# A fused attention, quantised feed-forward and expert kernel: the attention and expert stages written in new orders, and the first chunk's inputs loaded early

## The chip, the cores and the metric

One core of a Trainium2 chip runs the kernel. The metric is the device time of one execution in microseconds. A core has TensorE (PE, with its weight loads PEld), VectorE (DVE), ScalarE (ACT), GpSimd (POOL) and SyncE (SP). Each engine runs its own list of instructions strictly in the order written; they meet only at semaphores. SP issues all DMAs but a few of the setup.

## The reference

```python
x = x + tanh(g_xattn[0]) * L0_xattn(layernorm(x), ctx)      # 4 heads, one score matrix summed over the batch, |.| >= 1
x = x + tanh(g_ffn[0])   * L0_ffn(layernorm(x))             # rms_norm * gamma, int8-quantised rows, ternary weights, gelu
x = x + tanh(g_xattn[1]) * L1_xattn(ctx, ctx, layernorm(x)) # causal convolution of k*v pairs, times q, 64 groups of 8
x = x + tanh(g_ffn[1])   * L1_ffn(layernorm(x))             # top-6 routing, 6 experts and 2 shared ones, silu(g) * u
```

x and ctx are 16 x 256 x 512 in fp32 (4096 rows of 512), the first feed-forward widens to 2048, an expert to 256. In the first feed-forward a layer norm (mean m, variance v, epsilon 1e-5) is followed by an RMS norm with epsilon 1e-6.

## The kernel before

The 4096 rows are cut into 8 chunks of 512 (four tiles of 128 rows). Four stages follow each other, each in its own block, with all engines meeting between blocks: a setup; the scores stage (`scores_block`), which sums the score matrix over all chunks and writes gates and values of every chunk to DRAM; the attention stage (`attn_block`); the experts stage (`experts_block`). fp32 operands of a product are split in a high and a low part (tile names ending in `_hi`, `_lo`), and `products` (L52) issues three matmuls for one.

**Attention stage**, one chunk q: `retention` (values times scores, half s into `ps_o`), `group_stats`, `group_pow`, `group_shift`, `group_norm` (group norm, into `ao`), `turn_o` (transposes into `ps_r`), `times_gamma`, `gated`, `cut_z`, `project` (output product, `ps_r` again), `add_x` (residual), then for pairs of tiles `pair_variance`, `pair_rms`, `layer_pow`, `pair_shift`, `layer_norm`, `times_gain`, `pair_scale`, `round_y`, `pair_bf16` and a DMA transpose `turn_y`. For each tile j follow `mm1` (four products into three banks `ps_h`), `gelu` per bank, `scale_h` (row maximum), `round_h`, `to_bf16`, a DMA transpose `turn_h`, `mm2` (one bank `ps_y`), `residual` and `store`. The values' high parts are made by `cut_v` (ACT) and the low ones on POOL. Python loops write the stage out in full; in round c the engines work at the feed-forward of chunk c and, interleaved by hand, at the attention of chunk c + 1. The order in a round is the order of the calls, for instance on ACT (L714 to L731):

```python
            gelu(c, 2, (2, 3))
            ...
                for k in range(KT):
                    cut_z(q, k)
            round_h(c, 1)
            if q + 1 < NCH:
                cut_v(q + 1)
            round_h(c, 2)
            gelu(c, 3)
```

Variances are made by `variance` (L59): six small DVE operations on the even and odd halves that bn_stats leaves. `pair_rms` and a second power on POOL give the RMS factor.

**Experts stage**, one chunk q: `turn_x2`, `norm_x`, `turn_q`, `read_q` bring x in; `keys`, `pairs` (POOL), `cut_kv`, `cut_t` prepare 16 `unit`s of the convolution, whose products go to `ps_m` and are multiplied and reduced on DVE (`e_zp`, `e_x3T`); `add_x2`, `turn_x3`, `nat_stats`, `norm_nat`, `turn_xn`, `cut_xn` give the normalised input `e_xn`. Then come 16 steps s (4 shared, 12 routed) of `gate`, `up`, `silu`, `weigh`, `gated`, `cut_hd` and `down`; `gate` and `up` have one PSUM bank each, `down` sums over all steps in `ps_out`. `finish` and `store` end the chunk. Round g does the steps of chunk g and the convolution of chunk g + 1; the table `UNITS` says at which steps the units stand. Each engine's rounds stand in one `Fori` loop (L1167, L1254, L1454, L1661, L1843), so one copy of the code is run again, and DMA addresses and some operands are computed in registers. The first chunk's convolution stands ahead of the loop. The stage begins with the loads of its x, keys (`e_c`), filter (`e_t_raw`) and constants (L1135 to L1147).

## Time and profile before

| what | value |
|---|---|
| median of 3 runs | 2332.93 us (2327.42 to 2332.95) |
| profiled execution, its own time | 2325.81 us |
| its span, first to last instruction | 2324.0 us |
| granted TensorE clock, mean | 0.944 |
| busy share: PE, DVE, ACT, POOL | 87%, 67%, 44%, 41% |
| HBM traffic | 193.26 MB read, 33.69 MB written |

The span is the time from the first to the last instruction of the one profiled execution; the 1.8 us between it and its own time lie around it. Busy shares are means over four stages with different limits, so the stages have to be read apart.

### The profile page before, as it was taken

What the parts mean: (1) busy time and instruction counts of PE and PEld (TensorE: products, weight loads), DVE (VectorE), ACT (ScalarE), POOL (GpSimd) and SP (SyncE); (2) the same over time, 40 slices, a digit from 0 to 9 for tenths busy, and PEclk for the clock granted to TensorE, in tenths of its full rate; (3) what the DMA queues carried; (4) which work ended last, traced back from release to release, by engine and by line L of the source; (5) the groups of instructions that cost most, each with busy time, mean ns of one, the idle gap of its engine ahead of it and who ended that gap; (6) DMA issues with size and microseconds to landing.
All of it is one profiled execution on the core that took longest, in us unless ns stands there. A gap on an engine that the chain in (4) does not pass through costs nothing.

```text
span 2324.0 us, 30136 instructions
## 1 busy us (share of the span) xinstructions
PE 2017.0 (87%) x10162; PEld 1602.5 (69%) x10162; DVE 1546.4 (67%) x2487; ACT 1017.7 (44%) x1414; POOL 952.0 (41%) x775
## 2 busy tenths in 40 slices
PE   5999568887787545799899899899899899899998
PEld 4989444444454234688788788788788788688787
DVE  4776456666666358588578678678578579578511
ACT  3345345555555321633633633633633633443432
POOL 0110133333332021465465465465465465365464
PEclk9999779999999857899999999999999999899999
DMA  6666314443443321322332332332232242232231
GB/s 214 235 217 231 131 54 116 111 105 96 108 118 82 69 66 46 104 85 90 111 95 86 109 103 86 106 106 86 93 119 82 80 124 90 72 113 73 69 136 64
DMA packets 169968, 248.76 MB, mean 107 GB/s; under 512 B 91280, under 2 KB 92688, under 8 KB 163632
## 3 DMA queue, kind: packets, MB, share of 16 engines
q1 hardware_dynamic: 169616, 247.86, 34.3%
q8 instruction: 34, 0.56, 0.1%
q14 instruction: 30, 0.25, 0.0%
q10 hardware_dynamic: 288, 0.10, 0.0%
HBM read 193.26 MB, written 33.69 MB: 98 GB/s over the span
## 4 chain that ended last, share of the span: by engine, by line
PE 43%; DVE 7%; issue 6%; ACT 5%; POOL 3%; DMA 1%; ACTq 0%; SPq 0%; DVEq 0%; POOLq 0%
PE e_ps_u L54 4%; PE e_ps_u L56 4%; PE e_ps_u L55 4%; PE e_ps_m L54 4%; PE e_ps_m L56 3%; PE e_ps_m L55 3%; PE e_ps_out L54 3%; PE e_ps_out L55 3%; PE e_ps_out L56 3%; PE e_ps_g L56 3%; PE e_ps_g L55 3%; PE e_ps_g L54 3%; POOL e_dn_lo L1185 1%; DVE e_kv_lo L1504 1%; DVE e_x3T L1532 1%
## 5 line engine op out<-in xcount | busy, mean ns | idle before, releaser
L1180 POOL TENSOR_TENSOR e_gu_lo<-e_gu_raw,e_gu_hi 128x1024 fp32r<-128x1024 f32 (+1 forms) x128 | 272.8, 2131 | 449.6 <-ACT e_gu_hi L1269 447.3
L1532 DVE TENSOR_REDUCE e_x3T<-e_zp 128x128 f32<-128x1024 f32 x128 | 267.4, 2089 | 4.4
L54 PE MATMUL e_ps_u<-e_xn_hi,e_gu_hi 128*128 128x512 f32 x512 | 205.5, 401 | 4.0 <-DVE e_xn_lo L1554 2.5
L54 PE MATMUL e_ps_out<-e_hd_hi,e_dn_hi 128*128 128x512 f32 x512 | 208.8, 408 | 0.0
L54 PE MATMUL e_ps_m<-e_kv_hi,e_t_hi 128*128 128x288 f32 x592 | 180.7, 305 | 29.7 <-DVE e_kv_lo L1504 22.1
L55 PE MATMUL e_ps_out<-e_hd_lo,e_dn_hi 128*128 128x512 f32 x512 | 205.2, 401 | 0.0
L56 PE MATMUL e_ps_out<-e_hd_hi,e_dn_lo 128*128 128x512 f32 x512 | 205.2, 401 | 0.0
L55 PE MATMUL e_ps_u<-e_xn_lo,e_gu_hi 128*128 128x512 f32 x512 | 203.7, 398 | 0.0
L56 PE MATMUL e_ps_u<-e_xn_hi,e_gu_lo 128*128 128x512 f32 x512 | 203.6, 398 | 0.0
L958 PE MATMUL ps_h<-w1q,ayqT 128*128 128x512 bf16 x512 | 130.3, 403 | 79.4 <-ACT ah L681 71.9
L1203 POOL TENSOR_TENSOR e_kv_raw<-e_ke 128x512 f32<-128x512 f32 x128 | 139.4, 1089 | 125.7 <-DVE e_kv_lo L1504 95.5
L1185 POOL TENSOR_TENSOR e_dn_lo<-e_dn_raw,e_dn_hi 128x512 fp32r<-128x512 f32 x128 | 179.6, 1403 | 6.9 <-ACT e_dn_hi L1275 6.9
L1477 DVE TENSOR_TENSOR e_hd_lo<-e_hd,e_hd_hi 128x512 fp32r<-128x512 f32 x128 | 125.2, 978 | 78.6 <-ACT e_hd_hi L1297 78.6
L56 PE MATMUL e_ps_m<-e_kv_hi,e_t_lo 128*128 128x288 f32 x592 | 177.0, 299 | 0.0
L55 PE MATMUL e_ps_m<-e_kv_lo,e_t_hi 128*128 128x288 f32 x592 | 176.8, 299 | 0.0
L1283 ACT ACTIVATE e_sg<-e_ps_g,vecs 128x512 f32<-128x512 f32 x96 | 66.2, 690 | 242.4 <-PE e_ps_g L56 241.5
L1472 DVE SCALAR_TENSOR_TENSOR e_hd<-e_ps_u,vecs,e_sgw 128x512 f32<-128x512 f32 x96 | 71.7, 747 | 140.7 <-PE e_ps_u L56 116.0
L1297 ACT ACTIVATE e_hd_hi<-e_hd 128x512 fp32r<-128x512 f32 x128 | 80.4, 628 | 190.0 <-DVE e_hd L1472 189.7
L1194 POOL TENSOR_TENSOR e_sgw<-e_sg,e_wb 128x512 f32<-128x512 f32 x96 | 127.1, 1324 | 80.2 <-ACT e_sg L1283 79.5
L958 PEld LDWEIGHTS ps_h<-w1q,ayqT 128*128 128x128 bf16 x512 | 48.4, 101 | 151.1 <-ACT ah L681 87.5
L54 PE MATMUL e_ps_g<-e_xn_hi,e_gu_hi 128*128 128x512 f32 x384 | 152.5, 397 | 0.0
L56 PE MATMUL e_ps_g<-e_xn_hi,e_gu_lo 128*128 128x512 f32 x384 | 151.5, 395 | 0.0
(271 smaller groups left out, 5304.7 us busy)
## 6 DMA issues: line engine op xcount, KB each, us to landing
e_gu_raw<-in_mgu SPq DMA_DIRECT2D x96, 512.0 KB, 3.3
e_dn_raw<-in_md SPq DMA_DIRECT2D x128, 256.0 KB, 3.2
e_wb<-wts SPq DMA_DIRECT2D x8, 1536.0 KB, 6.6
stage<-in_x SPq DMA_DIRECT2D x8, 1024.0 KB, 6.8
c<-in_ctxT SPq DMA_DIRECT2D x8, 1024.0 KB, 5.8
raw_w<-in_w1T SPq DMA_DIRECT2D x8, 1024.0 KB, 4.8
raw_w<-in_w2T SPq DMA_DIRECT2D x8, 1024.0 KB, 7.3
gates<-gate SPq DMA_DIRECT2D x8, 1024.0 KB, 4.8
```

The lines of the kernel that those rows point to most:

```text
L54: nc.tensor.matmul(out, w_hi, x_hi, start=first, stop=False, skip_group_check=skip)
L55: nc.tensor.matmul(out, w_hi, x_lo, start=False, stop=False, skip_group_check=skip)
L56: return nc.tensor.matmul(out, w_lo, x_hi, start=False, stop=last, skip_group_check=skip)
L958: last = nc.tensor.matmul(h_bank(c, j, n)[:], yqT[:, j, k], keep["w1q"][:, k, n * 512:(n + 1) * 512], start=(k == 0), stop=(k == KT - 1))
L1180: nc.gpsimd.tensor_tensor(gu_lo[:, s % 2, a], gu_raw[:, s % 2, a], f32(gu_hi[:, s % 2, a]), ALU.subtract).then_inc(gulo_done, 1)
L1185: nc.gpsimd.tensor_tensor(dn_lo[:, s % 2], dn_raw[:, s % 2], f32(dn_hi[:, s % 2]), ALU.subtract).then_inc(dnlo_done, 1)
L1194: nc.gpsimd.tensor_tensor(sgw[:], sg[:], wb[:, (s - SHARED) // 2], ALU.mult).then_inc(sgw_done, 1)
L1203: nc.gpsimd.tensor_tensor(out[:, :, 0:32].rearrange("p b (d i) -> p b d i", i=CD), view(ke, m * B * EXT, (EXT, B), (0, 4), (1, CD)), view( ...
L1297: nc.scalar.activation(hd_hi[:, s % 2], hd[:], ACT.Copy).then_inc(hdhi_done, 1)
L1472: nc.vector.scalar_tensor_tensor(out=hd[:], in0=ps_u[:], scalar=vecs[:, V_BU + e:V_BU + e + 1], in1=sgw[:], op0=ALU.add, op1=ALU.mult).the ...
L1477: nc.vector.tensor_tensor(hd_lo[:, s % 2], hd[:], f32(hd_hi[:, s % 2]), ALU.subtract).then_inc(hdlo_done, 1)
L1532: nc.vector.tensor_reduce(x3T[:, lb].rearrange("p (b n) -> p b n", b=B)[:, :, hh * CD:(hh + 1) * CD], zv(5, (1, 8), (21, 8)), AX.X, ALU.ad ...
```

## The change

The scores stage keeps its code; its tiles `gate` and `val` now lie in buffers that live through the whole kernel.

- **Attention stage.** All five engines' lists are written anew, each as one loop over i of single calls in which `at(op, c, ...)` issues a call only for an existing chunk. The work of one iteration is taken from three chunks: PE does `mm2` of tiles 1 to 3 of chunk i - 1, `mm1` of chunk i, `turn_o` and `project` of chunk i + 1, and `retention` of chunk i + 2. Work on four tiles or pairs is split in single calls (`gelu` per bank, `layer_norm`, `round_y`, `times_gain` per tile).
- **Small operations.** `variance` is replaced by `bn_aggr` per tile and one tensor_scalar in the attention and experts stages (not in the scores stage). `pair_rms` and the second power go: the scale is ((1 + 1e-6) v + 1e-6 * 1e-5)^-0.5 in one power, v the variance without epsilon. `pair_scale` and `scale_h` lose one operation each.
- **Experts stage.** The `Fori` loops are gone; all rounds are written out, again as one loop over i of single calls. `down` of the last step moves behind the round's end, in front of the next round's `up`; `down_first` splits the first `down` by output block; units stand at other places between the steps; `finish` is called per output block; the DVE part of a unit is split in `multiply` and `add_terms`.
- **Early loads.** `stage`, `o` and `gate` are shared by the stages. In the attention stage's last rounds SP loads the first chunk's keys into `stage` once the last values are cut, its first filter and constants into `gate`, and three quarters of its x rows into `o`. The experts stage then loads only the last quarter, `wroute` and `skipD` before it starts.

```diff
@@ attention, SP
+        def fetch_context():
+            sp.wait_ge(vlo_done, START + NCH)
+            sp.dma_start(early(keep)[1], dram["ctxG"].rearrange("g (k p) n -> g p k n", p=P)[0]).then_inc(early_in, 16)
+        def fetch_constants():
+            rest = early(keep)[2]
+            sp.wait_ge(z_done, START + 4 * NCH)
+            sp.dma_start(rest[:, 0], dram["toep"][0]).then_inc(early_in, 16)
...
+        def fetch_x():
+            sp.wait_ge(oT_done, 4 * NCH)
+            sp.wait_ge(x2_out, START + 16 * TJ * (NCH - 2))
+            for j in range(TJ - 1):
+                sp.dma_start(early(keep)[0][:, j], x2_rows(dram, 0, j)).then_inc(early_in, 16)
@@ attention, DVE: group_stats
-            variance(nc, dve, ostats, omom, ove[:], GN_EPS, omom_done, 12 * q + 6 * s)
+            for b in range(2):
+                nc.vector.bn_aggr(omv[:, b], ostats[:, b]).then_inc(omom_done, 1)
+            dve.wait_ge(omom_done, 6 * q + 3 * s + 2)
+            nc.vector.tensor_scalar(ove[:], omv[:, :, 1], GN_EPS, None, ALU.add).then_inc(omom_done, 1)
@@ attention, PE
+        for i in range(-2, NCH + 1):
+            at(mm2, i - 1, 1)
+            for n in range(4):
+                at(mm1, i, 0, n)
+            at(mm2, i - 1, 2)
+            at(turn_o, i + 1, 0)
+            at(turn_o, i + 1, 1)
+            for n in range(3):
+                at(mm1, i, 1, n)
+            at(turn_o, i + 1, 2)
+            at(turn_o, i + 1, 3)
+            at(mm2, i - 1, 3)
+            at(retention, i + 2, 0)
+            at(mm1, i, 1, 3)
+            for n in range(4):
+                at(mm1, i, 2, n)
+            at(project, i + 1, 0)
+            at(project, i + 1, 1)
+            at(mm1, i, 3, 0)
+            at(mm1, i, 3, 1)
+            at(project, i + 1, 2)
+            at(project, i + 1, 3)
+            at(mm1, i, 3, 2)
+            at(mm2, i, 0)
+            at(mm1, i, 3, 3)
+            at(retention, i + 2, 1)
@@ experts, SP
+        def load_first():
+            sp.sem_inc(x_in, 16 * (TJ - 1))
+            sp.dma_start(x[:, TJ - 1], x2_rows(dram, 0, TJ - 1)).then_inc(x_in, 16)
...
@@ experts, PE
-        with nc.Fori(0, NCH - 1, engines=(mybir.EngineType.PE,), hint_back_edge=True) as g:
-            round_(g, g + 1)
-        round_(NCH - 1, None)
+        for i in range(-1, NCH + 1):
+            at(down, i - 1, 15)
+            at(turn_x2, i + 1, 0)
+            at(up, i, 0)
...
+            at(up, i, 15)
+            at(turn_xn, i + 1, 0)
+            at(down, i, 13)
+            at(bias, i)
+            at(turn_xn, i + 1, 1)
+            at(down, i, 14)
```

**ACT in the middle of an attention round**, first before (`ah` with `ps_h` is `gelu`, `ah<-ah` is `round_h`, `az` `times_gamma`, `az_hi` `cut_z`, `av_hi` `cut_v`, `ay<-ax` `layer_norm`, `ay<-ay` `round_y`), then in the change:

```order
L657 ACTIVATE az<-ps_r,vecs 128x512 x4
L681 ACTIVATE ah<-ps_h,adq 128x512 x2
L664 ACTIVATE az_hi<-az 128x512 x4
L686 ACTIVATE ah<-ah,arnd,ahscale 128x2048
L645 ACTIVATE av_hi<-stage 128x2048
L686 ACTIVATE ah<-ah,arnd,ahscale 128x2048
L681 ACTIVATE ah<-ps_h,adq 128x512 x4
```

```order
L691 ACTIVATE ah<-ps_h,adq 128x512 x5
L696 ACTIVATE ah<-ah,arnd,ahscale 128x2048 x2
L682 ACTIVATE ay<-ax,ashift,ascale 128x512 x2
L691 ACTIVATE ah<-ps_h,adq 128x512
L662 ACTIVATE o<-ps_o,aoshift,aorstd 128x512 x2
L691 ACTIVATE ah<-ps_h,adq 128x512 x2
L686 ACTIVATE ay<-ay,arnd,aqscale 128x512 x2
L691 ACTIVATE ah<-ps_h,adq 128x512
L682 ACTIVATE ay<-ax,ashift,ascale 128x512 x2
```

The third tile's four gelus now precede the two long `round_h`, the fourth tile's are spread one by one between other work, and `cut_v` has moved to the round's end.

**SP at the change of stage**, before and in the change (the two branches are the end of the attention block and the start of the experts block; `o`, `stage` and `gate_held` are the shared buffers):

```order
L1003 UNCONDITIONAL_BRANCH
L1088 UNCONDITIONAL_BRANCH
L1110 DMA e_x<-x 128x1x512 x4
L1115 DMA e_c<-in_ctxG 128x4x512
L1119 DMA e_t_raw<-in_toep 128x512
L1140 DMA e_hd<-in_bdown 96x512
```

```order
L965 UNCONDITIONAL_BRANCH
L1053 UNCONDITIONAL_BRANCH
L1072 DMA o<-x 128x1x512
L1075 DMA e_xnat<-in_wroute 128x4x8
L1076 DMA e_skip<-in_skipD 128x32
L1097 DMA gate_held<-in_toep 128x512 x4
```

One load of x and two small ones stand where nine loads stood; the others are 7 to 16 rows ahead of the branches, between the transposes of the last two chunks.

**ACT at the end of an experts round**, before and in the change (`e_xq` is `norm_x`, `e_xn_hi` `cut_xn`, `e_sg` `silu`):

```order
L1283 ACTIVATE e_sg<-e_ps_g,vecs 128x512
L1301 ISA
L1303 ACTIVATE e_xq<-e_x,e_shift,e_rstd 128x512 x4
L1356 ACTIVATE e_xn_hi<-e_ps_m 128x1024
L1293 REGISTER_ALU
L1297 ACTIVATE e_hd_hi<-e_hd 128x512
L1356 ACTIVATE e_xn_hi<-e_ps_m 128x1024
```

```order
L1292 ACTIVATE e_sg<-e_ps_g,vecs 128x512
L1308 ACTIVATE e_hd_hi<-gate_held 128x512
L1278 ACTIVATE e_gu_hi<-e_gu_raw 128x512
L1363 ACTIVATE e_xn_hi<-e_ps_m 128x1024
L1284 ACTIVATE e_dn_hi<-e_dn_raw 128x512
L1334 ACTIVATE e_ke<-stage 128x64x8
L1335 ACTIVATE e_ke<-stage 128x64x4
L1284 ACTIVATE e_dn_hi<-e_dn_raw 128x512
L1278 ACTIVATE e_gu_hi<-e_gu_raw 128x512
L1308 ACTIVATE e_hd_hi<-gate_held 128x512
L1363 ACTIVATE e_xn_hi<-e_ps_m 128x1024
L1314 ACTIVATE e_xq<-o,e_shift,e_rstd 128x512 x4
```

`norm_x`, which stood ahead of both `cut_xn`, now stands behind both, and the register instructions of the loop are gone.

## Rows read from the trace of the kernel before

**Rows 1.** Stretches: A:B length, busy (x) of PE PEld DVE ACT POOL, granted clock, DMA share, GB/s.
```profile
318.20:386.60 68.40, 53.78 (x241) 31.90 (x242) 44.47 (x106) 36.03 (x44) 22.78 (x19) 0.88 0.33 81
386.60:756.36 369.76, 297.27 (x1418) 177.25 (x1416) 243.65 (x560) 197.58 (x245) 110.78 (x90) 0.95 0.41 106
756.36:806.90 50.54, 33.39 (x129) 12.73 (x127) 22.41 (x36) 19.86 (x22) 0.18 (x2) 0.90 0.33 73
806.90:847.30 40.40, 9.60 (x38) 7.73 (x38) 8.09 (x19) 11.62 (x18) 6.24 (x9) 0.52 0.35 97
847.30:945.80 98.50, 52.99 (x267) 47.74 (x267) 82.28 (x135) 20.85 (x36) 23.83 (x34) 0.67 0.12 35
945.80:1126.00 180.20, 172.62 (x855) 144.34 (x856) 130.72 (x179) 84.15 (x127) 98.85 (x80) 0.96 0.27 88
1126.00:2187.50 1061.50, 1018.44 (x5143) 853.72 (x5142) 793.32 (x1086) 470.93 (x710) 583.24 (x471) 0.98 0.30 96
2187.50:2324.00 136.50, 126.77 (x550) 101.29 (x548) 30.07 (x51) 49.34 (x71) 66.35 (x42) 0.99 0.31 107
```

**Rows 2.** Waits of PE from 386.6 to 756.36: total us, times, longest.
```profile
PE ps_h L958 <- ACT ah L681: 52.9, 24, 4.4
PE ps_y L966 <- DVE ax L843: 16.9, 12, 3.9
```

**Rows 3.** Timeline of ACT and PE in one attention round: start, length, wait in brackets.
```profile
536.09 2.09 ACT L686 ACTIVATE ah<-ah,arnd,ahscale 128x2048 f32<-128x2048 f32 x1
538.07 1.91 ACT L645 ACTIVATE av_hi<-stage 128x2048 fp32r<-128x2048 f32 x1
539.87 2.09 ACT L686 ACTIVATE ah<-ah,arnd,ahscale 128x2048 f32<-128x2048 f32 x1
...
542.59 1.89 PE L958 MATMUL ps_h<-w1q,ayqT 128*128 128x512 bf16 x4 [4.39 <-ACT ah L681]
...
563.44 3.63 PE L966 MATMUL ps_y<-w2q,ahqT 128*128 128x512 bf16 x16 [1.07 <-DVE ax L843]
```

**Rows 4.** Waits of PE from 1126 to 2187.5.
```profile
PE e_ps_m L1765 <- DVE e_xn_lo L1554: 21.4, 5, 4.3
```

**Rows 5.** Timeline at the end of one experts round.
```profile
1465.28 1.04 PE L1765 MATMUL e_ps_m<-ident,e_xnat 128*128 128x128 f32 x8
...
1468.11 2.93 ACT L1303 ACTIVATE e_xq<-e_x,e_shift,e_rstd 128x512 f32<-128x512 f32 x4 [4.72 <-DVE e_shift L1488]
...
1471.97 1.22 DVE L1554 TENSOR_TENSOR e_xn_lo<-e_ps_m,e_xn_hi 128x1024 fp32r<-128x1024 f32 x1 [3.22 <-ACT e_xn_hi L1356]
...
1473.35 0.85 PE L1765 MATMUL e_ps_m<-ident,e_xnat 128*128 128x128 f32 x6 [4.25 <-DVE e_xn_lo L1554]
```

**Rows 6.** Timeline at the start of the experts stage.
```profile
807.66 2.69 SPq L1110 DMA_DIRECT2D e_x<-x  x4
...
824.44 2.47 DVE L1482 BATCH_NORM_STATS2 e_stats<-e_x 128x6 f32<-128x512 f32 x4 [20.38 <-DMA e_x<-x]
```

**Rows 7.** Small operations of a variance in the experts stage: ns min/median/max.
```profile
L63 DVE TENSOR_TENSOR e_pmom<-e_pstats x16: 146/150/155, 925.5 to 2168.1; 128x2 f32<-128x2 f32 x16
L64 DVE TENSOR_TENSOR e_pmom<-e_pstats x16: 154/1258/1262, 925.6 to 2168.1; 128x2 f32<-128x2 f32 x16
```

**Rows 8.** Groups of the attention rounds, 386.6 to 756.36: busy us, mean ns, idle before.
```profile
L767 DVE SCALAR_TENSOR_TENSOR ax<-ps_r,gains,ax 128x512 f32<-128x512 f32 x24 | 17.9, 748 | 43.5 <-PE ps_r L56 42.8
...
L770 DVE BATCH_NORM_STATS2 astats<-ax 128x6 f32<-128x512 f32 x24 | 16.7, 695 | 0.8
...
L802 DVE TENSOR_REDUCE aamax<-ay 128x2 f32<-128x1024 f32 x12 | 14.5, 1210 | 0.0
...
L675 ACT ACTIVATE ay<-ay,arnd,aqscale 128x512 f32<-128x512 f32 x24 | 18.2, 806 | 25.4 <-DVE aqscale L809 25.4
```

**Rows 9.** DMA transposes of `ayqT`, issue to landing.
```profile
DMA to landing us min/median/max: 3.0/3.1/4.8
```

**Rows 10.** DMA queues from 386.6 to 756.36: packets, MB, share of 16 engines.
```profile
q8 instruction: 11, 0.18, 0.2%
```

More of the change, by code:

```diff
@@ new lines, in _ @@
+        for i in range(-3, NCH):
+            at(gelu, i, 0, 0)
+            at(group_norm, i + 1, 1)
+            for n in range(1, 4):
+                at(gelu, i, 0, n)
+            at(round_y, i, 2)
+            at(round_y, i, 3)
+            at(times_gamma, i + 1, 0)
+            at(times_gamma, i + 1, 1)
+            at(gelu, i, 1, 0)
+            at(round_h, i, 0)
+            at(cut_z, i + 1, 0)
+            at(times_gamma, i + 1, 2)
+            at(cut_z, i + 1, 1)
+            at(times_gamma, i + 1, 3)
+            at(gelu, i, 1, 1)
+            at(cut_z, i + 1, 2)
+            at(gelu, i, 1, 2)
+            at(cut_z, i + 1, 3)
+            at(gelu, i, 1, 3)
+            for n in range(4):
+                at(gelu, i, 2, n)
+            at(round_h, i, 1)
+            at(round_h, i, 2)
+            at(layer_norm, i + 1, 0)
+            at(layer_norm, i + 1, 1)
+            at(gelu, i, 3, 0)
+            at(group_norm, i + 2, 0)
+            at(gelu, i, 3, 1)
+            at(gelu, i, 3, 2)
+            at(round_y, i + 1, 0)
+            at(round_y, i + 1, 1)
+            at(gelu, i, 3, 3)
+            at(layer_norm, i + 1, 2)
+            at(layer_norm, i + 1, 3)
+            at(cut_v, i + 3)
+            at(round_h, i, 3)
@@ new lines, in _ @@
+        for i in range(-2, NCH + 1):
+            at(pair_variance, i, 1)
+            at(residual, i - 1, 0)
+            at(to_whole, i, 0)
+            at(to_whole, i, 1)
+            at(pair_shift, i, 1)
+            at(scale_h, i - 1, 3)
+            at(group_stats, i + 1, 1)
+            at(residual, i - 1, 1)
+            at(group_shift, i + 1, 1)
+            at(to_bf16, i - 1, 3)
+            at(pair_scale, i, 1)
+            at(scale_h, i, 0)
+            at(residual, i - 1, 2)
+            at(gated, i + 1, 0)
+            at(to_whole, i, 2)
+            at(to_whole, i, 3)
+            at(gated, i + 1, 1)
+            at(to_bf16, i, 0)
+            at(gated, i + 1, 2)
+            at(gated, i + 1, 3)
+            at(residual, i - 1, 3)
+            at(group_stats, i + 2, 0)
+            at(scale_h, i, 1)
+            at(scale_h, i, 2)
+            at(add_x, i + 1, 0)
+            at(add_x, i + 1, 1)
+            at(group_shift, i + 2, 0)
+            at(pair_variance, i + 1, 0)
+            at(to_bf16, i, 1)
+            at(pair_shift, i + 1, 0)
+            at(to_bf16, i, 2)
+            at(add_x, i + 1, 2)
+            at(add_x, i + 1, 3)
+            at(pair_scale, i + 1, 0)
@@ L1847, in experts_block, with early, x2_rows @@
     st.close()
+def early(keep):
+    return keep["o"][:], keep["stage"][:], keep["gate"][:]
+def x2_rows(dram, q, j):
+    return dram["x2"].rearrange("(j b g r) d -> g j b r d", j=TJ, b=4, g=NCH)[q, j]
 def expert_constants(np):
```

1173 lines of the change are left out of this document (602 added, 571 removed).

## The prediction

> **What bounds the kernel now.** I read the stretches first [rows 1], then, in each, what PE waits for, since PE is busiest in all of them but one. The scores stage (to 259 us) and the setup keep their code, so nothing is expected there. In the attention stage six rounds run alike from 386.6 to 756.36: 61.6 us each, of which PE is busy 49.5, DVE 40.6, ACT 32.9 and POOL 18.5. No engine is full, so the order is the bound: PE waits 52.9 us for a gelu to free one of the three `ps_h` banks and 16.9 us for a residual to free the one `ps_y` bank [rows 2], 11.6 us a round. The largest of these waits, 4.39 us, has its reason on ACT: the fourth tile's gelus stand behind `round_h`, `cut_v` and another `round_h`, 2.09 + 1.91 + 2.09 us [rows 3]. In the experts stage the rounds take 180.2 us (the first) and 176.9 us (1061.5 / 6), with PE busy 172.6 and 169.7 [rows 1]: nearly full, 7 us idle. Of that 4.3 us is one wait a round, before the second `turn_xn` [rows 4]. There ACT does `norm_x`, itself late by 4.72 us, ahead of the `cut_xn` that PE wants [rows 5]. At the start of that stage all engines stand still from 806.9 to 824.4 us, until x has landed [rows 6]; then the first chunk's convolution runs alone, with DVE busy 82.3 of 98.5 us [rows 1].
>
> **The six attention rounds.** PE's work is unchanged in number. Its 49.5 us hold time at the lower clock: a mean granted clock of 0.95 means that a tenth of each round, 6 us, ran at 1.2 instead of 2.4 GHz, beside waits of up to 4.4 us; without these waits about 2 us of busy time go, which leaves a floor of 47.5. DVE loses 26 small operations a round (12 of 24 in four variances, six of `pair_rms`, two of `pair_shift`, two of `pair_scale`, four of `scale_h`) of 0.15 us [rows 7], 3 to 4 us: 37 remain. ACT's 32.9 and POOL's 18.5 stay below the floor too. So the question is whether the lists, run strictly in order, close at the floor. I walked the tightest ring: from the end of `project` of tile 3 to the next round's first `mm1`. Residual and statistics of that tile take 0.75 + 0.70, the pair's maximum and its small operations 1.21 + 0.5, two `round_y` 1.61, then on DVE a variance and a residual 1.0 and two conversions 0.9 [rows 8], the transpose 3.1 [rows 9], and some eight handovers together 1: 10.8 us. PE has meanwhile one `mm1` bank, `mm2`, another bank, a `retention` and another `mm2`. An `mm2` is 16 matmuls of 512 columns in 3.6 us [rows 3], so a bank with 4 takes 0.9, and the 24 of a `retention` with 256 columns about 2.7: 0.9 + 3.6 + 0.9 + 2.7 + 3.6 = 11.7 us. It closes with 0.9 us to spare, and with a transpose at the longest seen, 4.8, it misses by 0.8. The former reason for waiting is gone: the third tile's gelus now stand ahead of both `round_h`, and PE has `project` to do while those run. In the ring through `scale_h`, `round_h`, `to_bf16`, `turn_h` and `mm2` a whole round's order lies between making and using. I take 50.5 us, the floor and 3 us for what does not mesh: **6 x (61.6 - 50.5) = 67 us saved**. Bounds: 47.5 us (85 saved) and 56 us, half of the present idle kept (34).
>
> **The rest of the attention stage.** The first mm1 comes 1 us earlier, as the RMS steps go. From there to the next chunk's, 68.4 us [rows 1], PE was busy 53.8 and DVE 44.5; with the same order as later rounds, but chunk 1's attention begun earlier, I take 50: **18 saved** (6 to 24). The last chunk, 50.5 us, is a chain of gelu, maximum, rounding, transpose and `mm2` for the last tile, which no order shortens; **3 saved** (0 to 8). The new waits on SP are cheap there: `fetch_context` waits for the last `cut_v` on POOL, `fetch_constants` for the last `gated`, `fetch_x` for the last `turn_o`, and behind them stand `turn_h` of chunk 6 and `turn_y` of chunk 7. All three events come well before those transposes have their data. The 2.4 MB that are loaded there must share the DMA engines, whose share is 0.41 in these rounds; at most a few us, inside the bound. Together: **89 saved** (41 to 118).
>
> **Start of the experts stage.** Of nine loads ahead of the first work three are left. Before, four loads of x took SP from 807.66 to 810.35 to issue and had landed only at 824.4, in the company of 1 MB of keys and the constants [rows 6]. Now 256 KB come alone. A landing of 3 to 5 us, as the transposes show [rows 9], puts the statistics at about 812; but the DVE operations on constants that used to follow them now stand ahead of `norm_shift`, 4 us. **9 saved** (5 to 12). The convolution of the first chunk has the same DVE work in another order: **2 saved** (0 to 5).
>
> **The seven full experts rounds.** PE's 169.7 us of work stay. At the boundary ACT now does `cut_xn` first and `norm_x` after both, and PE has a `down` and the `bias`, 16 matmuls of 512 columns, 3.6 us, between the two `turn_xn`. The chain that it waits for is 0.9 for the high part (from the end of `norm_x` to the start of DVE's part), 1.22 for the low one and 0.5 for handovers [rows 5], 2.6 us. `down` of steps 14 and 15 cover the second half. The other waits are 3 us in sum, scattered over the units. In return the units stand at new places, and one PSUM bank each for gate, up and the units allows little disorder. I take 170.5 against a mean of 177.4: **48 saved**. Bounds: 168 (66) and 175.5 (13). The last round has PE busy 126.8 of 136.5 us, and its end is a fixed chain: **2 saved** (0 to 4).
>
> **bn_aggr** does not occur in the trace. Its bounds are the free small operation, 0.15 us, and the stretched one, 1.26 us, which is the median of the third operation of a variance in the experts stage, though it is identical in kind to the one at 0.15 [rows 7]. I take 0.16, since in each variance only the operations that meet POOL's work are stretched. There are eight a round in both stages; at 1.26 they would bring DVE from 37 to 46 us in an attention round, near PE's own time, and lead to the first rival below. [...]
>
> **The sum.** 89 + 9 + 2 + 48 + 2 = 150. Against the profiled execution's own 2325.8 us that gives 2175.8. The median shown is 7.1 higher than that execution, the lowest run 1.6; I add 4 and forecast **2180 us**. With all bounds at their ends together it is 2125 (205 saved) to 2271 (59 saved).
>
> **The rivals.** (1) *DVE or ACT takes PE's place in the attention rounds.* For it: 37 of 50.5 us on DVE, in a strict order with PE results between; against it: the ring above closes. With 57 us a round 28 instead of 67 are saved, and 8 instead of 18 in the first: 2229 us. Chance 0.15. (2) *The experts rounds' waits only move.* DVE and POOL block each other (1.26 for 0.15 us), and the new order may bring more of DVE's two-input cuts beside POOL's work while PE stands at a unit; at 176 us a round 10 are saved instead of 48: 2218 us. [...] Chance 0.15. (3) *Slower: the written-out rounds starve PE of instructions.* The attention rounds, which are written out, fetched 11 blocks for 1418 matmuls and 1416 weight loads [rows 1, 10], one per 258. The experts rounds, 6548 matmuls from 945.8 on and as many loads, would need 51 where a loop now repeats one copy. A block's packet takes 0.2% x 16 x 369.8 / 11 = 1.1 us; hidden, it costs nothing, and in the attention rounds PE's waits have other names. It decides from 150 / 51 = 2.9 us of standstill a block. At 4.8 us each, the longest landing in rows 9, it is 245 us: 2425 us. Chance 0.04. (4) *The change does not do what it says*, orders close no better than the present ones and the lost small operations were hidden: within 7 us of now. Chance 0.02.
>
> **How the numbers follow.** The forecast's case has 0.64. Its own range is 2130 to 2215. To hold eight in ten the range must take in rivals 1 and 2 singly but not their sum (2267): **2130 to 2255 us**. A measurement of this kernel tells 0.3% (7 us) from no change. Faster by more than that: the forecast and rivals 1 and 2, 0.94; within it 0.02; slower 0.04.
>
> **What would show it.** Attention: `mm2` to `mm2` a round of 50 us, PE's waits for gelu under 2 us a round, DVE near 37 us busy. Experts: e_stats 10 us earlier after the block's start, the wait before the second `turn_xn` gone, rounds near 170. Wrong would be: a new releaser of PE with over 4 us a round; bn_aggr over 1 us; PE idle by "issue" at regular distances; a `turn_y` held up on SP behind a store or a load, which would show as PE waiting for `ayqT`.

## The result, and the profile after

The changed kernel takes **2111.6 us** (median of 4 runs, 2109.9 to 2112.5) against 2332.7 for the kernel before, timed beside it (4 runs, 2327.4 to 2333.0). The ratio is 0.9056, 95% interval 0.9041 to 0.9072: **9.4% faster**. The direction was forecast and the size was not: 221 us were saved where I forecast 150, and 205 with every bound at its end together. 2111.6 lies below the forecast range of 2130 to 2255 us.

The profiled execution's own time is 2112.1 us (before 2325.8) and its span 2110.3 us (2324.0), so 213.7 us of span went. Here after's stretches stand, cut at the same events as [rows 1] and with the same columns (x is a count of instructions): length; busy time of PE, PEld, DVE, ACT and POOL; granted clock, DMA share, GB/s.

```profile
319.90:364.00 44.10, 41.78 (x208) 25.77 (x209) 38.56 (x64) 34.08 (x43) 19.50 (x14) 0.97 0.52 120
364.00:635.60 271.60, 271.46 (x1393) 168.18 (x1391) 236.32 (x398) 196.44 (x243) 118.71 (x76) 1.00 0.57 144
635.60:689.50 53.90, 36.98 (x160) 15.47 (x160) 24.12 (x34) 21.78 (x23) 0.46 (x2) 0.92 0.61 117
689.50:717.10 27.60, 9.68 (x40) 8.19 (x41) 8.15 (x19) 13.32 (x21) 8.65 (x13) 0.50 0.08 21
717.10:812.50 95.40, 53.26 (x274) 48.83 (x274) 78.93 (x125) 21.23 (x34) 23.09 (x32) 0.70 0.17 47
812.50:979.30 166.80, 166.80 (x859) 141.28 (x857) 122.66 (x173) 78.58 (x119) 101.84 (x78) 0.99 0.31 96
979.30:1975.60 996.30, 994.74 (x5131) 842.40 (x5130) 744.73 (x1044) 460.01 (x702) 609.35 (x472) 1.00 0.32 103
1975.60:2110.30 134.70, 127.19 (x553) 101.99 (x551) 40.82 (x51) 48.18 (x71) 68.25 (x41) 0.99 0.31 104
```

The second and the seventh row carry the result: PE is busy 271.46 of 271.60 us in six attention rounds and 994.74 of 996.30 in six experts rounds, at a granted clock of 1.00. Both stages now run at PE's own speed. Set against the forecast, part by part (before's last cut stands here at 2186.7, the first `up` of the last chunk, where [rows 1] have 2187.5):

| part | before | after | saved | forecast |
|---|---|---|---|---|
| to the first `mm1` | 318.2 | 319.9 | -1.7 | 1 |
| first attention iteration | 68.4 | 44.1 | 24.3 | 18 (6 to 24) |
| six attention rounds | 369.8 | 271.6 | 98.2 | 67 (34 to 85) |
| last chunk | 50.5 | 53.9 | -3.4 | 3 (0 to 8) |
| experts, start | 40.4 | 27.6 | 12.8 | 9 (5 to 12) |
| first convolution | 98.5 | 95.4 | 3.1 | 2 (0 to 5) |
| seven experts rounds | 1240.9 | 1163.1 | 77.8 | 48 (13 to 66) |
| last round and tail | 137.3 | 134.7 | 2.6 | 2 (0 to 4) |

The same events do not enclose quite the same work. After's first iteration holds 32 matmuls of `mm2` fewer than before's (x208 against x241 in all) and its last chunk 32 more (x160 against x129), 6.9 us at 0.216 us each; and the six rounds hold 24 matmuls of 256 columns fewer (2.9 us), since half a `retention` now comes earlier. Of the 1.7 us lost up to the first `mm1`, 1.6 lie ahead of the attention stage's first matmul, in stages whose code did not change.

The two large terms are each 30 us too small and beyond their bounds. In [rows 2] PE waited 69.8 us for a gelu or a residual; the waits of PE in after's six rounds are an empty list. In the six experts rounds, where [rows 4] show 21.4 us, one row is left (columns: total us, times, longest):

```profile
PE e_ps_m L1886 <- DVE e_x3T L1587: 1.6, 2, 0.8
```

Two things went against me. The last chunk became longer, by the two `mm2` moved there and by PE waiting for the transposes of `ahq`:

```profile
PE ps_y L933 <- DMA ahqT<-ahq: 12.1, 3, 8.3
```

and the prologue did not gain what its shorter arithmetic should give: 52.4 us from the first `retention` to the first `mm1` in both kernels. DVE and POOL there, from after's timeline (start, length, wait in brackets):

```profile
283.86 0.17 DVE L750 TENSOR_SCALAR aove<-aomv 128x2 f32<-128x2 f32 x1
284.85 4.44 DVE L755 SCALAR_TENSOR_TENSOR aoshift<-aomv,aorstd 128x2 f32<-128x2 f32 x1 [0.82 <-POOL aorstd L616]
...
284.11 0.71 POOL L616 TENSOR_TENSOR aorstd<-aove,amhalf 128x2 f32<-128x2 f32 x1 [8.99 <-DVE aove L750]
284.79 4.50 POOL L612 TENSOR_TENSOR av_lo<-stage,av_hi 128x2048 fp32r<-128x2048 f32 x1
```

An operation of two elements a partition took 4.44 us. It started 0.06 us after POOL's `av_lo` of chunk 1, which the new order puts there; that this is the reason is tested in e9.

### The profile page after: what moved, and what is told of

Same layout as the page of the kernel before. It is cut to its first block, busy times and chain, and to the rows that moved or that the text cites. A ratio compares the mean times of both kernels' runs of the same rounds, so it can differ in the third digit from the quotient of the medians.

```text
span 2110.3 us, 28277 instructions
## 1 busy us (share of the span) xinstructions
PE 1955.2 (93%) x10162; PEld 1580.1 (75%) x10162; DVE 1493.0 (71%) x2223; ACT 1005.8 (48%) x1403; POOL 992.6 (47%) x759
## 4 chain that ended last, share of the span: by engine, by line
PE 59%; DVE 4%; DMA 2%; issue 1%; SPq 1%; ACT 0%; POOL 0%; DVEq 0%; ACTq 0%
PE e_ps_u L54 5%; PE e_ps_u L56 5%; PE e_ps_u L55 5%; PE e_ps_out L54 5%; PE e_ps_out L55 5%; PE e_ps_out L56 5%; PE e_ps_g L54 4%; PE e_ps_g L56 4%; PE e_ps_g L55 4%; PE e_ps_m L54 3%; PE e_ps_m L55 3%; PE e_ps_m L56 3%; DMA e_dn_raw<-in_md 1%; DVE e_x3T L1581 1%; PE e_ps_m L1855 1%
## 5 line engine op out<-in xcount | busy, mean ns | idle before, releaser
L1165 POOL TENSOR_TENSOR e_gu_lo<-e_gu_raw,e_gu_hi 128x1024 fp32r<-128x1024 f32 (+1 forms) x128 | 285.3, 2231 | 176.7 <-ACT e_gu_hi L1278 176.7
L1170 POOL TENSOR_TENSOR e_dn_lo<-e_dn_raw,e_dn_hi 128x512 fp32r<-128x512 f32 x128 | 180.3, 1411 | 118.5 <-ACT e_dn_hi L1284 117.6
L1186 POOL TENSOR_TENSOR e_kv_raw<-e_ke 128x512 f32<-128x512 f32 x128 | 146.2, 1142 | 131.8 <-DVE e_kv_lo L1549 122.3
L54 PE MATMUL e_ps_out<-e_hd_hi,e_dn_hi 128*128 128x512 f32 x512 | 203.9, 398 | 0.0
L54 PE MATMUL e_ps_m<-e_kv_hi,e_t_hi 128*128 128x288 f32 x592 | 177.5, 300 | 17.5 <-DVE e_kv_lo L1549 10.7
L1519 DVE TENSOR_TENSOR e_hd_lo<-gate_held,e_hd_hi 128x512 fp32r<-128x512 f32 x128 | 145.0, 1133 | 68.3 <-ACT e_hd_hi L1308 68.1
L1177 POOL TENSOR_TENSOR gate_held<-e_sg,e_wb 128x512 f32<-128x512 f32 x96 | 138.3, 1441 | 115.3 <-ACT e_sg L1292 65.1
L1347 ACT ACTIVATE e_kv_hi<-e_kv_raw 128x576 fp32r<-128x576 f32 x128 | 85.9, 678 | 195.7 <-PE e_ps_m L56 92.5
L1565 DVE TENSOR_TENSOR e_zp<-e_ps_m,e_qe 128x512 f32<-128x512 f32 x120 | 82.7, 689 | 131.9 <-PE e_ps_m L56 131.7
L1284 ACT ACTIVATE e_dn_hi<-e_dn_raw 128x512 fp32r<-128x512 f32 x128 | 79.3, 626 | 179.4 <-PE e_ps_out L56 153.1
L1278 ACT ACTIVATE e_gu_hi<-e_gu_raw 128x1024 fp32r<-128x1024 f32 (+1 forms) x128 | 120.8, 944 | 78.1 <-issue 44.1
L55 PE MATMUL e_ps_g<-e_xn_lo,e_gu_hi 128*128 128x512 f32 x384 | 151.3, 394 | 0.0
```

Source lines behind the costliest of these rows:

```text
L54: nc.tensor.matmul(out, w_hi, x_hi, start=first, stop=False, skip_group_check=skip)
L55: nc.tensor.matmul(out, w_hi, x_lo, start=False, stop=False, skip_group_check=skip)
L1165: nc.gpsimd.tensor_tensor(gu_lo[:, s % 2, a], gu_raw[:, s % 2, a], f32(gu_hi[:, s % 2, a]), ALU.subtract).then_inc(gulo_done, 1)
L1170: nc.gpsimd.tensor_tensor(dn_lo[:, s % 2], dn_raw[:, s % 2], f32(dn_hi[:, s % 2]), ALU.subtract).then_inc(dnlo_done, 1)
L1177: nc.gpsimd.tensor_tensor(sgw[:], sg[:], wb[:, (s - SHARED) // 2], ALU.mult).then_inc(sgw_done, 1)
L1186: nc.gpsimd.tensor_tensor(out[:, :, 0:32].rearrange("p b (d i) -> p b d i", i=CD), view(ke, m * B * EXT, (EXT, B), (0, 4), (1, CD)), view( ...
```

## The experiments

My theory after reading this: the rounds are bound by PE's issue, the orders close with nothing left over, and my floor for PE was read from the wrong column. Rivals: the gain of a stage owes something to the other stage, to the written-out loops, or to the dropped small operations rather than to the order.

**One stage at a time (e1, e2, e3).** e1 has after's attention stage without its early loads and before's experts stage; e2 has before's attention stage and after's experts stage with the eight early loads back at its start, beside the three that stayed; e3 is after without early loads:

```
-            if i == NCH - 1:
-                fetch_context()
...
-            sp.sem_inc(x_in, 16 * (TJ - 1))
-            sp.dma_start(x[:, TJ - 1], x2_rows(dram, 0, TJ - 1)).then_inc(x_in, 16)
-            sp.sem_inc(c_in, 16)
-            sp.sem_inc(t_in, 16)
+            for j in range(TJ):
+                sp.dma_start(x[:, j], x2_rows(dram, 0, j)).then_inc(x_in, 16)
+            sp.dma_start(c[:], dram["ctxG"]...[0]).then_inc(c_in, 16)
+            sp.dma_start(t_raw[:], dram["toep"][0]).then_inc(t_in, 16)
...
```

> The attention stage of the changed kernel without its early loads, and the experts stage of before word for word. Theory (the attention's gain is its own, rounds of 45.3 us because PE never waits): 2333 less 24 for the first iteration, 98 for six rounds and 3 for the last chunk, about 2208 us; six rounds of 45.3 us with PE waiting under 1 us a round; the last chunk 47 to 48 us instead of 53.9, since no load stands before its transposes. Rival (the rounds owe part of their gain to something outside the attention's orders): rounds of 47 us or more, 2220 us and up.

> The attention stage of before word for word, and the experts stage of the changed kernel with all its loads at the stage's start. Theory (PE-bound rounds of 166.2 us whatever comes before): 2333 less 78 for seven rounds, 3 for the first convolution and 3 for the last round, about 2249 us; the stage's start near 40 us as before. Rival (the granted clock or the early loads are behind part of it): rounds over 168 us, 2262 us and up.

> The changed kernel with nothing loaded ahead of the experts stage: the eight loads stand at its start. Theory: the stage's start goes back from 27.6 to some 38 us (+11), the last chunk from 53.9 to 48 us (-6), so 2116 to 2120 us against 2111.6. Rival (the last chunk's wait for transposes has nothing to do with the loads): the last chunk stays at 53 to 54 us and the whole is 2122 us or more.

Measured: e1 2191.9 us (0.9401, interval 0.9385 to 0.9416), e2 2243.3 (0.9624, 0.9604 to 0.9644), e3 2114.0 (0.9066, 0.9050 to 0.9081). e1's six rounds and last chunk, and two of e2's experts rounds:

```profile
362.70:634.50 271.80, 271.42 (x1393) 168.18 (x1391) 236.59 (x398) 196.88 (x243) 118.84 (x76) 1.00 0.56 138
634.50:675.00 40.50, 35.36 (x160) 15.29 (x160) 23.02 (x33) 21.65 (x23) 0.18 (x1) 1.00 0.56 126
```
```profile
1278.80:1610.50 331.70, 331.70 (x1715) 281.10 (x1714) 249.24 (x353) 154.82 (x236) 204.52 (x159) 1.00 0.33 105
```

Each stage keeps its rounds whatever stands beside it (45.3 and 165.9 us), so that rival falls. Yet e1 came out 16 us and e2 6 us below what I expected. In e1 a part of it is the last chunk: from its first `mm1` to the end of its last `mm2` it takes 40.5 us in e1, 46.9 before and 50.3 in after; the new order does shorten it, even with two `mm2` more in it, and the early loads more than took that back. The rest is before's own: its median in these comparisons is 4 to 7 us above its profiled execution, and its trace has 5 us that e1's does not have (below, e4). In e3, without early loads, the start is 11 us longer than in after (20.2 us from the last `mm2` to the first PE work, against 9.0) and the last chunk 9.8 us shorter. So loading ahead was worth 1.4 us in the traces and 2.4 in the medians, and the two intervals overlap: no gain clear of noise, where I forecast 9.

**The loops written out (e4).** In before:

```
-        with nc.Fori(0, NCH - 2, engines=(mybir.EngineType.Activation,), hint_back_edge=True) as g:
+        for g in range(NCH - 2):
             round_(g, g + 1, True)
```

and the same for SP, POOL and DVE.

> Before with the four hardware loops of the experts stage on SP, POOL, ACT and DVE written out, and nothing else changed; PE's loop stays. Theory (the gain of the experts stage is the order's): the same within 5 us of 2333, rounds of 176 to 178 us, the wait before the second turn_xn still about 4.3 us. Rival (the jump back of a loop cost a part of each round's idle 7 us): rounds of 173 us or less, 2310 us or less. Other rival (fetching instructions costs time): rounds over 180 us.

Measured 2322.8 us (0.9962, 0.9948 to 0.9976), 9 us faster, where I expected 5 at most. The rounds themselves gained nothing: 177.2 to 177.6 us, where before's loop took 175.9 to 177.8, and the wait for `e_xn_lo` is 4.1 us each. The one gain in the trace is in the round after the loop's last pass: 170.7 us against 176.0 before; the rest of the 9 us is, as in e1, before's median above its trace. In that round PE waits once for ACT in before, and ACT for nothing that the profile shows. PE's wait (total us, times, longest):

```profile
PE e_ps_g L1778 <- ACT e_sgw L1361: 4.1, 1, 4.1
```

ACT's timeline:

```profile
2015.43 0.63 ACT L1297 ACTIVATE e_hd_hi<-e_hd 128x512 fp32r<-128x512 f32 x1
2020.64 0.59 ACT L1361 ACTIVATE e_sgw<-e_ps_g 16x512 f32<-16x512 f32 x1 [4.59 <-issue]
```

and the second instruction queue from 2010 to 2025 us (packets, MB, share):

```profile
q14 instruction: 2, 0.02, 0.3%
```

The two packets of that queue fall into the stretch in which ACT leaves its loop; from 1080 to 2010 us, inside the loops, no instruction packet moved at all. The pause is there in every run that keeps the loops, 4.5 to 4.6 us, once: on ACT in before, e5, e7 and e8, on DVE in e1, where PE did not come to wait for it; and it is in neither run that writes them out (e4, e13). So leaving a loop cost one engine 4.5 us once and PE up to 4.1, and passing its end cost nothing that can be seen. The Trainium skill, page "Runtime: NRT & Kernel Launch", section "Instruction fetch mechanics", says that a taken branch to a target outside the two blocks held stalls until the block has come; the wait at the exit fits that. That the exit is such a branch no run shows, and that the packets are what ACT waited for is their place in time (the first started 1.6 us before ACT went on), not an experiment.

**The small operations (e5, e6, e13).** e5 is before with the attention's small operations in the new form and its order kept; e6 is after with the old form and its order kept; e13 is e4 with `bn_aggr` in the experts stage. The core of e5's edit, and of e6's with the signs turned:

```
-            variance(nc, dve, stats[:, cols], mom[:, :, cols], ve[:, cols], LN_EPS, mom_done, 12 * q + 6 * a)
+            for j in (2 * a, 2 * a + 1):
+                nc.vector.bn_aggr(mv[:, j], stats[:, j]).then_inc(mom_done, 1)
+            dve.wait_ge(mom_done, 6 * q + 3 * a + 2)
+            nc.vector.tensor_scalar(ve[:, cols], mv[:, cols, 1], 1.0 + RMS_EPS, RMS_EPS * LN_EPS, ALU.mult, ALU.add)...
...
-                pair_rms(q, 0)
```

> Before with the attention's small operations in the new form (bn_aggr pairs, one power, a step instead of a clipped maximum), its order kept and its experts stage as before. Theory (the order sets the attention's time): DVE loses 3 to 4 us a round, PE's waits for gelu stay above 6 us a round, rounds of 59.5 to 61 us instead of 61.6: 2315 to 2327 us. Rival (the removed operations lay on the path): 4 us a round and more, eight rounds and the prologue, below 2300 us.

> The changed kernel with the attention's small operations in the old form (26 more a round on DVE, a second power on POOL), its order kept. Theory (PE is the bound, and the new order has room on DVE): DVE goes from 39.4 to about 43 of 45.3 us, the rounds grow by 0 to 1 us, the prologue by 1 to 2: 2112 to 2122 us. Rival (DVE is the next bound at once): rounds of 48 us or more, 2130 us and up.

> The kernel of e4 (before, loops of the experts stage written out) with bn_aggr in place of the six-operation variance in the experts stage's three norms, its order kept; to be read against e4's 2322.8 us. Theory (there the removed operations are on the path, as in the attention stage: nat_stats stands between two groups of transposes, and the shift that norm_x waits 4.72 us for comes out of a variance): 2 to 4 us a round, 2295 to 2309 us. Rival (they are hidden, and the experts stage's gain is the order's alone): rounds stay at 177.4, within 4 us of 2322.8.

Measured: e5 2295.9 us (0.9856, 0.9839 to 0.9872), e6 2128.6 (0.9142, 0.9127 to 0.9157), e13 2303.4 (0.9878, 0.9863 to 0.9894), 19.4 below e4. In e5 my theory fell: the rival's 4 us a round came. The waits of PE in e5's six rounds, 380.2 to 727.3:

```profile
PE ps_h L943 <- ACT ah L678: 42.1, 24, 4.4
PE ps_y L951 <- DMA ahqT<-ahq: 6.9, 5, 1.7
PE ps_y L951 <- DVE ax L831: 3.6, 2, 2.7
```

and the stretch itself:

```profile
380.20:727.30 347.10, 291.84 (x1418) 175.17 (x1417) 218.13 (x404) 197.49 (x245) 101.33 (x77) 0.97 0.44 113
```

The gelu waits of [rows 2] shrink from 52.9 to 42.1 us and those for the residual from 16.9 to 3.6, with 6.9 new ones for a transpose; 57.9 us a round instead of 61.6. In the new order the same operations are worth less, though more than I expected (e6 lies between my theory's 2122 and the rival's 2130). Its six rounds:

```profile
367.20:652.70 285.50, 275.69 (x1393) 166.76 (x1391) 261.05 (x556) 197.30 (x243) 127.94 (x89) 1.00 0.54 139
```

and PE's largest wait in them:

```profile
PE ps_r L919 <- ACT az L672: 6.9, 5, 1.4
```

285.5 / 6 = 47.6 us, 2.3 above after, and no engine is full (DVE 43.5). So of the 16.3 us that a round lost, the order gives 12.6 to 14.0 (0.5 of them by the half `retention` that left these rounds) and the small operations 2.3 to 3.8. In the experts stage they are worth 3.3 of 11.2 us: rounds of 173.3 to 174.6 us in e13, 174.1 in the mean, against e4's 177.4 and after's 166.2.

**One call moved (e7, e8).** In before, on ACT; e7:

```
-                if ahead and s == STEPS - 1:
-                    norm_x(q + 1)
                 if q is not None and s == STEPS - 1:
                     cut_xn(q, 0)
...
                     cut_xn(q, 1)
+                if ahead and s == STEPS - 1:
+                    norm_x(q + 1)
```

and e8:

```
-            round_h(c, 2)
             gelu(c, 3)
+            round_h(c, 2)
```

> Before with one call moved: ACT's norm_x of the next chunk behind both cut_xn. Theory (the wait before the second turn_xn is norm_x's): that wait falls from 4.3 to under 1 us in each of the rounds that have one, 15 to 26 us in all: 2307 to 2317 us. Rival (the wait only moves, since everything that norm_x feeds comes 3 us later): within 5 us of 2332.

> Before with one call moved: ACT's gelus of the fourth tile ahead of round_h of the third. Theory (one swap frees the ps_h bank but makes to_bf16 of the third tile late, with add_x, project and mm2 behind it, so the whole order had to change): rounds of 60 us or more, 2320 to 2345 us. Rival (this position alone was the fault): the wait of 4.4 us goes in every round, 57 us, about 2302 us.

e7: 2302.4 us (0.9881, 0.9864 to 0.9897), 27 us faster, a little more than my theory gave. Its rounds inside the loop take 172.7 to 172.9 us, against 176.9 in the mean before, and of the wait of [rows 4] this is left:

```profile
PE e_ps_m L1765 <- DVE e_xn_lo L1554: 4.7, 5, 1.0
```

My theory counted the wait alone, and the traces show what it left out. The six rounds before and in e7:

```profile
1126.48:2186.70 1060.22, 1017.16 (x5138) 852.67 (x5136) 792.72 (x1085) 470.45 (x710) 581.96 (x469) 0.98 0.30 96
```
```profile
1125.20:2162.70 1037.50, 1006.74 (x5132) 842.54 (x5131) 795.24 (x1084) 473.32 (x713) 586.16 (x470) 1.00 0.31 98
```

Over the six rounds PE stands idle 12.3 us less (43.1 to 30.8) and is also busy 10.4 us less for the same matmuls (1017.2 to 1006.7). In before the granted clock is at 1.2 GHz in six stretches, 34.1 us in all, and each begins within 1.4 us of the end of a wait of over 4 us (five before the second `turn_xn`, one at the loop's exit). In e7 only the wait at the exit is left of these, and there are two such stretches, 6.8 us together, one of them at that wait.

e8: 2327.1 us (0.9985, 0.9976 to 0.9995), 2.6 us faster. The gelu wait goes from 52.9 to 46.8 us in six rounds, the longest from 4.4 to 3.4, and the rounds stay at 62.0 (61.6 before). PE is idle 5.7 us less there and busy 8.1 us more, for in this trace the time at 1.2 GHz is 51.2 us against 34.1. In the experts stage one call was the fault of 4.2 us a round; in the attention stage the one that I moved is not, and the order as a whole did it.

**More work for PE (e12).** In after, one matmul more ahead of each bank of `mm1`, its result overwritten:

```
+            nc.tensor.matmul(h_bank(c, j, n)[:], yqT[:, j, 0], keep["w1q"][:, 0, n * 512:(n + 1) * 512], start=True, stop=True)
             for k in range(KT):
```

> The changed kernel with one more bf16 matmul of 512 columns ahead of each bank of mm1 (16 a chunk, 128 in all), whose result is overwritten. Theory (PE is the bound and its price is the distance from start to start, 0.216 us): 3.46 us a round, the rounds go from 46.1 to 49.6 us, 24 to 28 us in all: 2136 to 2139 us. Rival (the busy column is the price and there is slack in it): 1.5 us a round or less, below 2124 us.

Measured 2136.3 us (0.9168, 0.9151 to 0.9184), 24.7 above after. Its six rounds:

```profile
364.70:656.50 291.80, 291.71 (x1489) 177.74 (x1487) 236.69 (x398) 197.09 (x242) 118.65 (x76) 1.00 0.52 135
```

20.2 us more for 96 matmuls, 0.210 us each. That is the distance from start to start (0.216 us), not the 0.38 us that the busy column gives one of them, and no slack swallowed it; PE still waits for nothing there. PE is the bound, and this is its price.

**The two losses (e9, e10, e11, e14).** In after: e9 makes POOL's first `av_lo` of chunk 1 wait for the shift; e10 moves `fetch_x` behind the last `turn_h`; e11 does both and lets ACT read PE's first block of transposes before `norm_x`; e14 is e11 with the three loads one by one behind `turn_h` of tiles 0, 1 and 2 of the last chunk.

```
 e9           def cut_v(q):
                  pool.wait_ge(vhi_done, q + 1)
+                 if q == 1:
+                     pool.wait_ge(oshift_done, 2)
 e10          at(turn_h, i - 2, 3)
+             if i == NCH + 1:
+                 fetch_x()
              at(store, i - 2, 0)
 e11  +       read_x2T(0, 0)
              for i in range(-2, NCH):
                  at(norm_x, i + 1)
```

> The changed kernel with one wait more, once: POOL begins the low part of chunk 1's values only when DVE has made the shift of chunk 0's second group norm. Theory (the 4.44 us of that shift, 2 elements wide, are DVE shut out by POOL's 4.50 us of av_lo): the shift takes under 0.5 us, the first turn_o and all behind it come 3.5 to 4.3 us earlier: 2107 to 2108.5 us. Rival (the shift is late for another reason, or the retention that then comes later takes the gain back): within 1 us of 2111.6.

> The changed kernel with the three early loads of x moved on SP behind the last turn_h, all other early loads where they are. Theory (these 768 KB hold up the transposes of the last two chunks): the last chunk falls from 50.3 us to 41 to 43, the start of the experts stage stays at 9 to 11 us from the last mm2 to the first PE work: 2101 to 2104 us. Rival (the load of the context and the constants holds them up, or x then lands later than the experts stage wants it): 2109 us or more.

> The changed kernel with both edits of e9 and e10 and a third: ACT reads the first two transposed blocks of x of chunk 0 before its norm_x and right behind it, where PE waited 7.96 us for e_x2T. The third alone should give 3 us before the first multiply, if PE's chain of four groups of transposes sets the start of the convolution, and 0 if DVE does. Sum of the three: 4 + 9 + 3, 2096 us; if the third gives nothing, 2099; rival (they do not add): 2103 us or more.

> The kernel of e11 with the three loads of x one by one, behind turn_h of tiles 0, 1 and 2 of the last chunk. Theory (in e10 and e11 the stage's last stores stood in the queues behind 768 KB, which is why the start of the experts stage grew from 9.0 to 14.2 us): the last chunk stays at 40 to 42 us, the start falls to 9 to 10: 2094 to 2097 us. Rival (each piece holds up the next transposes as the three did together): the last chunk at 44 us or more, 2099 us and up.

| | us | ratio to before (interval) | last chunk | last `mm2` to first PE work |
|---|---|---|---|---|
| after | 2111.6 | 0.9056 (0.9041 to 0.9072) | 50.3 | 9.0 |
| e9 | 2109.1 | 0.9050 (0.9034 to 0.9066) | 53.5 | 9.0 |
| e10 | 2106.3 | 0.9038 (0.9022 to 0.9054) | 40.3 | 14.4 |
| e11 | 2099.8 | 0.9016 (0.9001 to 0.9031) | 40.3 | 14.2 |
| e14 | 2098.7 | 0.9003 (0.8990 to 0.9015) | 42.8 | 9.1 |

e9's timeline of DVE and POOL, the low part now behind the shift:

```profile
283.89 0.16 DVE L757 SCALAR_TENSOR_TENSOR aoshift<-aomv,aorstd 128x2 f32<-128x2 f32 x1 [0.82 <-POOL aorstd L618]
...
284.20 4.51 POOL L614 TENSOR_TENSOR av_lo<-stage,av_hi 128x2048 fp32r<-128x2048 f32 x1 [0.34 <-DVE aoshift L757]
```

4.44 us became 0.16, and the first `mm1` came 4.0 us earlier after the first `retention` (48.5 against 52.4 us). In the median 2.5 us are left, less than I expected, and e9's interval overlaps after's. Its last chunk is 3.3 us longer with the same waits (12.2 and 12.1 us for transposes): there the granted clock is 0.87 against 0.93, and PE is busy 40.2 us instead of 37.0 for the same 160 matmuls. First after, then e9:

```profile
635.65:685.90 50.25, 36.98 (x160) 15.47 (x160) 23.32 (x33) 21.73 (x23) 0.38 (x1) 0.93 0.64 120
```
```profile
631.34:684.85 53.51, 40.15 (x160) 16.23 (x160) 23.30 (x33) 21.73 (x23) 0.38 (x1) 0.87 0.61 113
```

e10 shows that x's 768 KB held up the transposes: 10.0 us off the last chunk, with the context and the constants loaded early as before. Of these, 8.3 are waits for `ahq` (12.1 to 3.8) and 1.6 the clock, 1.00 there. But 5.4 us came back at the border. SP issued the last loads and stores as follows (e10):

```profile
668.87 2.05 SPq L578 DMA_DIRECT2D o<-x  x3
670.96 5.07 SPq L582 DMA_DIRECT2D x<-ax  x4
683.76 0.53 SPq L1072 DMA_DIRECT2D o<-x  x1
```

The attention stage waits for its last store and for the early loads to land before SP goes on. From the end of that store's issue this took 2.3 us in after (687.04 to 689.35) and takes 7.7 here (676.03 to 683.76): x had landed at 680.6, the store behind it at 683.1. e14 confirms that half: with the loads spread, the border is at 9.1 us again. And it half fails, for each piece holds up the next transpose (7.2 us of waits in e14, 3.8 in e10 and e11), and 2.5 us of the last chunk are lost. The third edit gave 1.4 us (117.6 to 116.2 us from the first PE work to the first `up`), not the 3 I expected. **e14 is the fastest kernel here, 0.6% below after.** Its interval and e11's are clear of after's; e10's overlaps after's, and e14's overlaps e11's, so between those nothing is decided by the totals.

## Why the prediction was wrong in size

**The step that failed: "which leaves a floor of 47.5", and the 3 us on top.** I took PE's floor from its busy time, 297.27 / 6 = 49.5 us a round, less 2 for the lower clock. The price is read from start to start. In one of after's rounds:

```profile
410.16 3.62 PE L925 MATMUL ps_h<-w1q,ayqT 128*128 128x512 bf16 x16
413.61 3.62 PE L933 MATMUL ps_y<-w2q,ahqT 128*128 128x512 bf16 x16
417.07 1.04 PE L903 MATMUL ps_r<-ident,o 128*128 128x128 f32 x8
```

16 matmuls take 3.45 us, 0.216 each, though they are shown as 3.62 long. The same medians were in before's trace: 768 bf16 matmuls of 512 columns at 0.216, 288 fp32 ones at 0.227, 264 of 256 columns at 0.120 and 96 transposes at 0.109 us in six rounds are 273.4 us, 45.6 a round. The 297.3 us busy are these and 23.9 more, 4.0 a round, of which I took off 2. Read start by start, they are two things. 16.1 us are wider distances, 15.3 of them in the ten stretches (34.1 us together) in which the granted clock was at 1.2 GHz. 7.8 us are the ends of the last matmuls before 48 stops: such an end lies under the next start when PE goes on, and counts in full when it stops. So the clock term was 2.7 us a round and not 2, and the ends, which I put at nothing, 1.3. Both go with the waits: in after's rounds, at 1.00 throughout, they are 0.4 and 0.5 us in all six. After runs 45.3, below 45.6, because half a `retention` left its six rounds (0.5 us a round); its own count gives 45.1.

So the floor was 2 us too high, and "3 us for what does not mesh" was next to nothing: my own ring closed with 0.9 us to spare, and I charged 3 all the same. 5.2 us a round, 31 us.

The experts stage is the same error, in "PE's 169.7 us of work stay". The medians over its six rounds add up to 993.3 us, 165.5 a round, and the busy time is 4.0 above it: 2.3 at the lower clock, 0.9 ends before waits and the rest other wider distances. I took off 1.7 for the bound of 168 and forecast 2.5 above that; after runs 165.9 in most rounds and 166.2 in the mean. 4.3 us a round, 30 us. e7 shows the clock's part with one call moved, and e12 confirms that the spacing is what PE charges.

**First iteration**: 24.3 saved, 18 forecast, the bound of 24 just passed. But 6.9 us of it are two `mm2` that moved to the last chunk; on like work it is 17.4, close to the forecast.

**What bounded the rounds** was right: the order, with PE's waits for gelu and residual, and `norm_x` ahead of `cut_xn` (e7 shows that one alone). But I priced the 26 dropped operations as DVE's busy time only and at nothing for the path. e5 shows 3.8 us a round on the path in the old order, e6 2.3 in the new. That a sum of busy times lies below the floor says nothing about a chain.

**Last chunk**: "a chain of gelu, maximum, rounding, transpose and `mm2` for the last tile, which no order shortens" was wrong by its order (6.4 us shorter in e1, with two `mm2` more in it) and "at most a few us" wrong by its loads (9.8 us in e3, 10.0 in e10). I looked at when the new waits on SP would be over, not at what the loads behind them do to transposes that queue with them. The sign I named, PE waiting for `ayqT`, was the wrong transpose: it waited for `ahqT`.

**Start of the experts stage**: 12.8 saved for 9, with early loads that cost as much in the last chunk as they gave here. Eleven loads stood ahead of the first work, not nine; three are left. x was there 5.5 us after its issue (689.35 to 694.86), a little above the 3 to 5 taken from [rows 9]; the statistics begin 5.4 us into the stage instead of 17.5, and the DVE operations on constants, charged with 4 us, took 2.8 (697.86 to 700.63). **The sum** also carried 4 us for before's median over its trace; it was 7, and after has none.

**The rivals.** DVE or ACT as the next bound: no; DVE is busy 39.4 of 45.3 us, 2.6 of them in the stretched `astep` of the last section. Moved waits in the experts rounds: no, 1.6 us in six rounds. Instructions: the six experts rounds fetched 42 blocks on the queue of [rows 10], and none of PE's waits there is for instructions:

```profile
q8 instruction: 42, 0.69, 0.3%
```

`bn_aggr` at 0.16 us was right: over the 32 of the group norms it took 148 ns at least, 166 in the median and 183 at most, with POOL at work beside half of them, though never with its long `av_lo`.

What stays open: e7 (4.2 us) and e13 (3.3) together would leave 3.7 us a round of the experts' 11.2, if they add, and neither was run with the other. That the rest lies in the places of the units is not shown; I did not test them by themselves. In the attention stage the order was tested only as a whole.

## What to carry to other kernels

Read the floor of a matmul stage from the distance between starts in stretches without waits, count times median, and never from the busy column of a stage that waits: that column also holds the ends before the waits and the matmuls at the lower clock around them, and both go when the waits go. When calls move across the edge of a stretch, count the instructions in it before calling a shorter stretch a gain. If a hand-walked ring closes, take the floor itself and let the chance, not the number, carry the doubt. A load moved early is paid for where it runs: ask which transposes or stores queue with it, and put a large one behind the last that PE waits for, or in pieces between them; here the two came out alike (2099.8 and 2098.7 us).
